# Running the context stage and the mamba projections of a four-layer cross-attention kernel in turns on each engine

## Chip, cores and metric

The kernel runs on one core of one Trainium2 chip. The metric is device time in microseconds (us) of that core; times of one execution come from its hardware profile.

## What is computed

Four layers run one after another on x (4 batches, 512 positions, width 256), all reading the same context ctx (4, 512, 256). In the first, a mamba block stands ahead of the attention. Cut to what matters here:

```python
# L0, mamba block: DI = 512, 8 heads of 64, state 128, convolution over 4 positions
zxbcdt = rms(x, norm_w) @ in_proj_w                  # 256 -> 512 (z) + 768 (xBC) + 8 (dt)
dt  = softplus(dt_raw + dt_bias)
xBC = silu(conv_b + sum(padded[:, k:k + L] * conv_w[:, k] for k in range(4)))
h_t = exp(dt * A) * h + (dt * xh) B_t ;  y_t = h_t C_t + D_skip * xh
x   = x + rms(y * silu(z), gnorm_w) @ out_proj_w
# L0..L3, cross attention: keys and values of each layer from ctx
#   L0: ctx @ Wk, ctx @ Wv   L1: the same kind   L2: ln(ctx)*g+b   L3: ln(ctx)*g1+beta1
# then L3's recurrence s = silu(s A') + u over 512 positions, plus mean(probs) @ W_prog'
```

## The kernel before

One program is written by hand for each engine: blocks for SyncE (L320), POOL (L364), ScalarE (L428), VectorE (L700) and TensorE (L1061). Each engine does its instructions in the order written, and named semaphores join them; so the order of the work is the order of these programs. Work is tiled in 16 tiles (NT) of 128 positions: 4 batches (NB) by 4 chunks (NCH). Stages stand one behind the other:

- Start. SyncE loads the first part of the packed weights (par0, the context weights), the four context blocks, the four x blocks, and then the other two parts of the weights (par_rest). POOL loads the mask and probs. TensorE takes the mean of probs (L1068) and its product (L1072); VectorE makes three bf16 parts of the mask row (L705 to L715) and the row of the mean (L717). Only then does TensorE begin the context (it waits for mod_dve 7). SyncE copies the mask parts into 12 rows (L334).
- Context, 16 tiles. TensorE turns the raw tile and the normalized one (L1094, through the helper at L1077), and makes all layers' keys (proj_T, L1084) and values (proj, L1091). ScalarE evacuates the turned tiles (ctx_ev, L435) and part of the keys and values (ctx_rows, L447); VectorE norms the context two tiles ahead (ctx_norm, L735; its root is taken by POOL, L376), and evacuates the rest (L743, L752). SyncE stores keys and values to HBM from two buffers. In between VectorE squares and scales the rows of x (L759, L772) and at tile 8 folds norm weights into projection weights (weights, L779). A tile uses four PSUM banks, two tiles all eight. The turn of a tile waits for c_dve, VectorE's last copy of two tiles before.
- Projections and convolution, 24 items: for each batch six groups of 128 channels by 512 positions. The normalized x is turned (L1137), copied by both engines (L471, L811), multiplied by the weights (L1160, into eight banks in turn), and after two items all 16 tiles' time steps are made in one run of matmuls 8 columns wide (L1146). For each item ScalarE copies it into a padded buffer (L491) and multiplies by the last tap (L492), VectorE adds the three other taps (L854), ScalarE applies SiLU (L483). There are NF = 5 buffers. VectorE makes the softplus of all time steps (L814 to L842) after three items.
- Scan over 16 chunks of tiles (L1163 on for TensorE, L500 to L547 for ScalarE, L857 to L899 for VectorE): ScalarE masks dt*A (L502), TensorE makes the decays (L1176), ScalarE exponentiates (the first use is L513), and so on.
- Attention for all layers, then the recurrence. Ahead of it POOL clears the pads of four value buffers (L400), and SyncE starts loading keys and values when that is done.

Of the kernel before, what the change touches and what calls it, by code (L numbers as in the profile page):

```python
# [8 lines left out]
BF16 = mybir.dt.bfloat16  # L9
# [5 lines left out]
P = 128  # L15
NB = 4
# [153 lines left out]
def build(nc, x, ctx_in, probs, maskf, pack, kd, vd, out):  # L170
    with ExitStack() as stack:
# [30 lines left out]
        XT = CX[:, :, :].rearrange("p a d -> p (a d)").rearrange("p (k b t) -> p k b t", k=KD, b=NB)  # L202
# [20 lines left out]
        arena = sb("arena", [P, 17920])  # L223
# [11 lines left out]
        a0 = Carve(arena[:, :])  # L235
        NX = a0.take(NT * D).rearrange("p (a d) -> p a d", a=NT)
        KS = [a0.take(KG * P).rearrange("p (g n) -> p g n", g=KG) for _ in range(2)]
        VS = [a0.take(VW) for _ in range(2)]
        cT = [[a0.take(KD * P).rearrange("p (k n) -> p k n", k=KD) for _ in range(3)] for _ in range(2)]
        cn = [a0.take(D) for _ in range(2)]  # L240
        keep = a0.take(T)
        pb = a0.take(NB * NCH * S3).rearrange("p (b k s) -> p b k s", b=NB, k=NCH)
        early = a0.take(6 * T)[0:1, :]
        m_row = early[:, 0:T]
        m_tmp = early[:, T:4 * T].rearrange("p (i n) -> p i n", i=3)
        m_part = early[:, 4 * T:6 * T].bitcast(BF16)[:, 0:3 * T].rearrange("p (i n) -> p i n", i=3)
# [6 lines left out]
        NF = 5  # L253
        xpad = [a1.take(T + CONV - 1) for _ in range(NF)]
        acc = [a1.take(T) for _ in range(NF)]
        dts = UTraw[:, 0:12 * NT * HM].rearrange("p (i a h) -> p i a h", i=12, a=NT)
# [3 lines left out]
        a2 = Carve(arena[:, rest:])  # L260
# [21 lines left out]
        Vs = [a3.take(NCH * (D + 16)).rearrange("p (k n) -> p k n", k=NCH) for _ in range(4)]  # L282
# [17 lines left out]
        ident = w("ident")  # L300

# [19 lines left out]
        def _(sp):  # L321
            sp.dma_start(W[:, CUTS[0]:CUTS[1]], pack[:, CUTS[0]:CUTS[1]]).then_inc(sem("par0"), 16)
            for b in range(NB):
                sp.dma_start(CX[:, b * NCH:(b + 1) * NCH, :], ctx_in[b].rearrange("(k p) d -> p k d", p=P)
                             ).then_inc(sem(f"cin{b}"), 16)
            for b in range(NB):
                sp.dma_start(res_by_b[:, :, b, :], x[b].rearrange("(k p) d -> p k d", p=P)
                             ).then_inc(sem(f"xin{b}"), 16)
            for i in range(1, 3):
                sp.dma_start(W[:, CUTS[i]:CUTS[i + 1]], pack[:, CUTS[i]:CUTS[i + 1]]).then_inc(sem("par_rest"), 16)  # L330
            sp.wait_ge(sem("mod_dve"), 6)
            for i in range(3):
                for g in range(4):
                    sp.dma_start(m_rows[32 * g + i:32 * g + i + 1, :], m_part[0:1, i, :]).then_inc(sem("mask_rows"), 16)  # L334

            for k in range(NT):
# [3 lines left out]
                sp.dma_start(vd[b, :, kt, :], VS[k % 2]).then_inc(sem(f"c_st{k % 2}"), 16)  # L340
            for s in range(2):
# [23 lines left out]
        def _(pool):  # L365
            pool.dma_start(keep.bitcast(I32), maskf.partition_broadcast(P)).then_inc(sem("early_in"), 16)
            pool.dma_start(m_row[:, :].bitcast(I32), maskf.rearrange("(a n) -> a n", a=1)).then_inc(sem("early_in"), 16)
            pool.dma_start(pb, probs.rearrange("b (k p) s -> p b k s", p=P)).then_inc(sem("early_in"), 16)
            pool.memset(Hst[:, :, :], 0.0)
            pool.memset(R2[:, :, :], 0.0)  # L370
            pool.memset(at2[:, :], 0.0)
            pool.memset(ones_b[:, :], 1.0).then_inc(sem("zeroed"), 1)

# [5 lines left out]
            for k in range(NT + 2):  # L379
                if k < NT:  # L380
                    root(st[k % 2][:, 9:10], st[k % 2][:, 8:9], "c", k + 1)
                if k >= NCH and (k - 2) % NCH == NCH - 1:
# [7 lines left out]
            for i in range(2):  # L390
                pool.wait_ge(sem(f"c_st{i}"), 32 * NT // 2)
# [1089 lines left out]
```

## Time and profile before

| | |
|---|---|
| median of 3 runs | 1637.56 us (1636.14 to 1640.12) |
| the profiled execution, its own time | 1636.14 us |
| its span | 1634.3 us |
| busy share of the span | TensorE 87%, ScalarE 68%, VectorE 65%, POOL 4% |
| mean granted TensorE clock | 0.944 of full speed |
| context stage | about 21 to 148 us |
| projections and convolution | about 148 to 230 us |
| scan | about 230 to 430 us |

A profile row names engine (PE is TensorE's matmuls, PEld its weight loads, DVE VectorE, ACT ScalarE, SP SyncE), line, operation and the tiles written and read. An fp32 matmul of the program shows as two records. "xN" is a number of instructions. In brackets stands the idle time of the engine ahead of a row and who ended it.

### The profile page before, as it was taken

To read this page: it belongs to the slowest core of one execution; us is meant where nothing else is said; L and a number is where in the kernel's file an instruction comes from. 1 tells how busy PE (TensorE), PEld (TensorE's weight loads), DVE (VectorE), ACT (ScalarE), POOL (GpSimd) and SP (SyncE) were. 2 spreads that over 40 slices of the span, in tenths; PEclk is the share of its full clock that TensorE was granted. 3 is DMA by queue.
4 is the path that set the end of the run, shared out by engine and by line. 5 is a ranking of instruction groups with operands and counts; after the bars stand their busy time and mean duration, and the time that the engine had idled before them with its cause. 6 is when DMAs were issued, how large, how long until landed. Compare 5 with 4: busy or idle time off the path is not lost.

```text
span 1634.3 us, 35969 instructions
## 1 busy us (share of the span) xinstructions
PE 1418.8 (87%) x13354; PEld 1031.5 (63%) x13354; DVE 1065.0 (65%) x2382; ACT 1114.4 (68%) x3382; POOL 64.6 (4%) x121
## 2 busy tenths in 40 slices
PE   5888939999789988999988999998889999888666
PEld 4787425666566655667766667776666777666444
DVE  2344776666477877867777776777777687777100
ACT  2343667888577888777778767778777777887322
POOL 1010000000100000000000000000000000000000
PEclk9999869999799999999999999999999999999655
DMA  9342000000212202212111221211022121010000
GB/s 330 115 133 93 0 0 0 2 0 1 103 41 76 69 27 64 86 38 75 54 43 37 68 64 40 66 53 53 27 79 66 40 79 53 27 53 2 7 20 26
DMA packets 67677, 90.43 MB, mean 55 GB/s; under 512 B 3440, under 2 KB 56688, under 8 KB 67120
## 3 DMA queue, kind: packets, MB, share of 16 engines
q1 hardware_dynamic: 67248, 87.34, 16.7%
q8 instruction: 108, 1.77, 0.5%
q0 software_dynamic: 256, 0.79, 0.2%
q14 instruction: 65, 0.53, 0.1%
HBM read 71.33 MB, written 16.78 MB: 54 GB/s over the span
## 4 chain that ended last, share of the span: by engine, by line
PE 58%; ACT 18%; DVE 12%; issue 10%; DMA 1%; POOL 1%; ACTq 0%; DVEq 0%; POOLq 0%
PE ps L1077 14%; PE ps L1318 10%; PE ps L1344 8%; PE ps L1084 7%; PE ps L1091 6%; DVE arena L1018 4%; PE ps L1303 3%; PE ps L1383 3%; ACT arena L639 3%; ACT dAm L502 2%; PE ps L1176 2%; DVE arena L854 2%; ACT arena L646 1%; ACT L608 1%; ACT R L698 1%
## 5 line engine op out<-in xcount | busy, mean ns | idle before, releaser
L1077 PE MATMUL ps<-W,arena 128*128 128x128 f32 x2928 | 439.2, 283 | 31.5 <-ACT arena L639 17.7
L1077 PEld LDWEIGHTS ps<-W,arena 128*128 128x128 f32 x2928 | 335.4, 148 | 180.0 <-issue 132.0
L639 ACT ACTIVATE arena<-ps,nmax 128x512 f32<-128x512 f32 x640 | 434.3, 685 | 2.1 <-DVE nmax L998 1.6
L646 ACT COPY arena<-ps 128x512 f32<-128x512 f32 x320 | 187.0, 584 | 212.7 <-PE ps L1077 208.5
L998 DVE TENSOR_REDUCE nmax<-ps 128x1 f32<-128x512 f32 x320 | 206.2, 686 | 122.0 <-PE ps L1318 82.3
L1018 DVE COPY arena<-ps 128x512 f32<-128x512 f32 x320 | 213.9, 687 | 24.2 <-PE ps L1077 11.1
L1318 PE MATMUL ps<-W,arena 32*128 32x512 f32 x1280 | 184.7, 645 | 34.8 <-DVE arena L1018 34.2
L1344 PE MATMUL ps<-arena 128*32 128x128 f32 x5120 | 172.9, 276 | 31.8 <-ACT arena L646 31.6
L1001 DVE TENSOR_REDUCE nmax<-ps 128x2 f32<-128x1024 f32 x160 | 193.8, 1211 | 0.0
L1344 PEld LDWEIGHTS ps<-arena 128*32 128x32 f32 x5120 | 130.0, 109 | 69.2 <-ACT arena L646 59.2
L1084 PE MATMUL ps<-arena,W 128*128 128x128 f32 x1152 | 153.2, 284 | 6.2 <-ACT arena L561 5.7
L1091 PE MATMUL ps<-W,arena 128*128 128x256 f32 (+1 forms) x608 | 148.5, 379 | 4.0 <-ACT arena L602 3.3
L1084 PEld LDWEIGHTS ps<-arena,W 128*128 128x128 f32 x1152 | 140.6, 197 | 12.5 <-ACT arena L561 11.6
L1303 PEld LDWEIGHTS ps<-R,at 128*128 128x128 f32 x768 | 115.6, 190 | 46.5 <-DVE R L981 25.1
L1303 PE MATMUL ps<-R,at 128*128 128x4 f32 x768 | 128.5, 238 | 6.2 <-DVE R L981 6.1
L639 ACT ACTIVATION_READ_ACCUMULATOR arena<-ps,nmax 128x1 f32 x640 | 130.4, 204 | 0.0
L1091 PEld LDWEIGHTS ps<-W,arena 128*128 128x128 f32 x608 | 104.0, 192 | 21.2 <-issue 6.1
L981 DVE SCALAR_TENSOR_TENSOR R<-th,ps 64x4 f32<-64x4 f32 x384 | 56.9, 148 | 88.9 <-ACT th L631 84.4
L376 POOL TENSOR_TENSOR st<-st,W 128x1 f32<-128x1 f32 x80 | 43.9, 548 | 1158.5 <-DVE st L727 1158.5
L1318 PEld LDWEIGHTS ps<-W,arena 32*128 32x128 f32 x1280 | 53.7, 185 | 52.1 <-issue 39.8
L631 ACT ACTIVATE th<-ps 64x4 f32<-64x4 f32 x384 | 64.0, 167 | 15.4 <-PE ps L1303 13.6
L1383 PE MATMUL ps<-R,W 64*64 64x4 f32 x256 | 47.5, 254 | 30.8 <-ACT R L698 30.8
(201 smaller groups left out, 1522.0 us busy)
## 6 DMA issues: line engine op xcount, KB each, us to landing
W<-keys SPq DMA_DIRECT2D x48, 512.0 KB, 3.7
arena<-values SPq DMA_DIRECT2D x48, 512.0 KB, 4.8
keys<-arena SPq DMA_DIRECT2D x16, 448.0 KB, 3.3
values<-arena SPq DMA_DIRECT2D x16, 448.0 KB, 3.9
W<-keys SPq DMA_DIRECT2D x16, 256.0 KB, 2.8
arena<-values SPq DMA_DIRECT2D x16, 256.0 KB, 3.2
W<-in_pack SPq DMA_DIRECT2D x1, 3180.0 KB, 18.1
W<-in_pack SPq DMA_DIRECT2D x1, 2246.0 KB, 10.1
```

The costliest lines, as they stand in the source:

```text
L639: nc.scalar.activation(Pr[:, a, :], ps[:, a, :], ACT.Exp, bias=nmax[:, u % 32:u % 32 + 1], accum_out=den[:, u % 32:u % 32 + 1]).then_inc(s ...
L646: nc.scalar.copy(PT[:, (4 * Q + a) % 8, :, :].rearrange("p k n -> p (k n)"), psT).then_inc(sem("u_ev_act"), 1)
L998: nc.vector.tensor_reduce(nmax[:, (u + g) % 32:(u + g) % 32 + 1], ps[:, g, :], AX, ALU.max, negate=True).then_inc(sem("u_mx"), 1)
L1001: nc.vector.tensor_reduce(nmax[:, u % 32:u % 32 + 2], ps[:, 2:4, :], AX, ALU.max, negate=True).then_inc(sem("u_mx"), 1)
L1018: nc.vector.tensor_copy(PT[:, (4 * Q + a) % 8, :, :].rearrange("p k n -> p (k n)"), ps[:, a, :]).then_inc(sem("u_ev_dve"), 1)
L1077: ins = nc.tensor.transpose(dst[:, k * P:(k + 1) * P], src[:, k * P:(k + 1) * P], ident)
L1084: ins = mm(dst[:, g * P:(g + 1) * P], w(wname, KD)[:, kk, g * P:(g + 1) * P], src[:, kk, :], start=kk == 0, stop=kk == KD - 1)
L1091: ins = mm(dst, src[:, kk, :], w(wname, parts)[:, kk, at_col:at_col + n], start=kk == 0, stop=kk == parts - 1)
L1303: mm(psR[:, NB * j:NB * (j + 1)], at2[:, :], R2[:, j, :], start=False, stop=True, skip_group_check=True).then_inc(sem("r_z"), 1)
L1318: ins = mm(ps[:, g, :], qT[b][rows, q, :], Ks[G % 4][rows, l.key_group(q), :], start=True, stop=l is not L0)
L1344: ins = mm(psT[32 * g:32 * g + 32, 0:P], Vs[G % 4][:, kt, first:first + 32], PT[:, (4 * Q + g) % 8, kt, :], start=kt == 0, stop=kt == NCH - 1)
L1383: mm(psR[0:S3, NB * j:NB * (j + 1)], W[0:S3, a3:a3 + S3], R2[0:S3, j, :], start=False, stop=True, skip_group_check=True).then_inc(sem("e_z ...
```

## The change

The context stage and the projections become one stage. In each engine's loop over the 16 context tiles, tile k = 4b + at carries a piece of batch b: at 0 the turn of the normalized x of that batch (half between the tile's keys and values, half behind the values), at 1 to 3 two items each, one in either place. The time steps of a batch stand behind the tile with at = 1, in four runs in place of one. PSUM is dealt anew: three banks for each of two context sides, and banks 6 and 7 (item) for the items. The turn of a tile waits for c_act (ScalarE's value copy) and no longer for c_dve. The norm weight mnorm is applied when the turned x is evacuated, no longer to the weights. NF is 4. The context's buffers move into the space of the attention weights, which are loaded after the last context store (par_late); VectorE's preparations from them (late_weights) stand at chunk 8 of the scan. The first context block is loaded before par0. Probs are loaded on SyncE's queue and summed by POOL, and the mean and its product stand behind tiles 2 and 3; the mask parts are made in tile 3. The softplus stands in tiles 14 and 15, in the last one between two convolutions. The value buffers lose their pads, and POOL's memset of them goes.

```diff
@@ SyncE
-            sp.dma_start(W[:, CUTS[0]:CUTS[1]], pack[:, CUTS[0]:CUTS[1]]).then_inc(sem("par0"), 16)
-            for b in range(NB):
-                sp.dma_start(CX[...], ctx_in[b]...).then_inc(sem(f"cin{b}"), 16)
...
+            load_ctx(0)
+            sp.dma_start(W[:, CUTS[0]:CUTS[1]], pack[:, CUTS[0]:CUTS[1]]).then_inc(sem("par0"), 16)
+            load_x(0)
+            sp.dma_start(W[:, CUTS[1]:CUTS[2]], pack[:, CUTS[1]:CUTS[2]]).then_inc(sem("par1"), 16)
+            load_ctx(1)
+            load_x(1)
+            sp.dma_start(pb, probs.rearrange("b (k p) s -> p b k s", p=P)).then_inc(sem("pb_in"), 16)
+            for b in range(2, NB):
+                load_ctx(b)
+                load_x(b)
...
+                if k == 3:
+                    sp.wait_ge(sem("mod_dve"), 6)
...
+            sp.dma_start(W[:, CUTS[2]:CUTS[3]], pack[:, CUTS[2]:CUTS[3]]).then_inc(sem("par_late"), 16)
             sp.wait_ge(sem("m_x1"), NT)
-            sp.wait_ge(sem("zeroed"), 3)
@@ POOL
+            for k in range(NT):
+                if k + 2 < NT:
+                    c_root(k + 2)
+                if k % NCH == NCH - 1 and k + 1 < NT:
+                    x_root(k // NCH + 1)
+                if k == 0:
+                    sum_probs()
+                if k == 4:
+                    pool.wait_ge(sem("mod_mm"), 1)
+                    pool.memset(Hst[:, :, :], 0.0).then_inc(sem("zeroed"), 1)
...
-            for v in Vs:
-                ins = pool.memset(v[:, :, P:], 0.0)
-            ins.then_inc(sem("zeroed"), 1)
@@ ScalarE
             ctx_ev(0)
             for k in range(NT):
+                if k:
+                    keep_item(k - 1, 1)
                 if k + 1 < NT:
                     ctx_ev(k + 1)
-                ctx_rows(k)
...
+                if k:
+                    silu(k - 1, 0)
+                ctx_keys(k)
+                if k % NCH == 0:
+                    keep_xT(k // NCH)
+                keep_item(k, 0)
+                if k:
+                    silu(k - 1, 1)
+                ctx_values(k)
+                if k == NT - 2:
                     act.wait_ge(sem("m_soft"), 3)
                     nc.scalar.activation(dts[:, 3, :, :], dts[:, 2, :, :], ACT.Exp).then_inc(sem("m_exp"), 1)
+                    nc.scalar.activation(negA[:, :], w("alog"), ACT.Exp).then_inc(sem("m_exp"), 1)
...
             act.wait_ge(sem("m_soft"), 19)
             masked_dA(0)
+            keep_item(NT - 1, 1)
+            silu(NT - 1, 0)
+            silu(NT - 1, 1)
@@ VectorE
+            ctx_norm(0)
+            ctx_norm(1)
...
+            for c in range(NCH):
+                x_square(c)
+            x_rows(0)
+            dve.wait_ge(sem("par1"), 16)
+            dve.wait_ge(sem("zeroed"), 2)
+            for k in range(NT):
+                b, at = divmod(k, NCH)
+                if k == NCH:
+                    mod_rows()
+                if at == 1:
+                    keep_xT(b)
+                if at == 2:
+                    time_steps(b)
+                ctx_keys(k)
+                if k + 2 < NT:
+                    ctx_norm(k + 2)
+                if k:
+                    conv(k - 1, 1)
+                if k == 3:
+                    mask_parts()
+                if k == NT - 2:
+                    softplus_front()
+                if k == NT - 1:
+                    softplus()
+                conv(k, 0)
+                if at == NCH - 1 and b + 1 < NB:
+                    x_square(NCH * (b + 1) + at)
+                    ctx_values(k)
+                    x_rows(b + 1)
+                else:
+                    ctx_values(k)
+                    if b + 1 < NB:
+                        x_square(NCH * (b + 1) + at)
+                if k == NT // 2:
+                    out_weights()
+            conv(NT - 1, 1)
@@ VectorE, scan
+                if k == NT // 2:
+                    late_weights()
@@ TensorE
             def ctx_turn(k):
-                    pe.wait_ge(sem("c_dve"), k - 1)
+                    pe.wait_ge(sem("c_act"), k - 1)
...
+            def items(k, j):
+                b, at = divmod(k, NCH)
+                if at == 0:
...
+                    for c in range(NCH):
+                        ins = nc.tensor.transpose(item[j][:, c * P:(c + 1) * P], NX[:, c, j * P:(j + 1) * P], ident)
+                    ins.then_inc(sem("xt_tp"), 1)
+                    return
+                f = number(item_of(k, j))
+                if at == 1:
+                    pe.wait_ge(sem("xt_act"), b + 1)
...
+                else:
+                    pe.wait_ge(sem("m_fa"), f - 1)
...
+                for kk in range(KD):
+                    ins = mm(item[j], inw[:, kk, DI + g * P:DI + (g + 1) * P], XT[b][:, kk, :], start=kk == 0, stop=kk == KD - 1)
+                ins.then_inc(sem("m_in"), 1)
...
             ctx_turn(0)
             for k in range(NT):
                 if k + 1 < NT:
                     ctx_turn(k + 1)
-                ctx_project(k)
+                ctx_keys(k)
+                items(k, 0)
+                ctx_values(k)
+                items(k, 1)
+                if k % NCH == 1:
+                    time_steps(k // NCH)
...
-                    if k == 0:
-                        pe.wait_ge(sem("m_silu"), NB * XG)
+                    if k < NB:
+                        pe.wait_ge(sem("m_silu"), XG * (k + 1))
```

## Rows read from the trace of the kernel before

**Rows 1.** Stretches: length, busy PE, PEld, DVE, ACT, POOL, clock, DMA share, GB/s.

```profile
40.00:60.00 20.00, 17.45 (x125) 15.60 (x124) 7.30 (x27) 8.19 (x24) 2.11 (x3) 1.00 0.37 122
200.00:220.00 20.00, 7.90 (x17) 2.60 (x15) 19.36 (x28) 16.05 (x27) 0.00 (x0) 0.83 0.00 0
220.00:240.00 20.00, 7.67 (x19) 4.84 (x20) 9.30 (x15) 11.43 (x25) 0.00 (x0) 0.50 0.00 0
```

**Rows 2.** Timeline of the start: start us, us, engine, line, operation.

```profile
14.48 3.55 PE L1068 MATMUL ps<-W,arena 128*64 128x1 f32 x32 [14.48 <-DMA arena<-in_probs]
14.79 0.41 DVE L705 TENSOR_SCALAR arena<-arena 1x512 f32<-1x512 int32 x1
...
17.56 0.41 DVE L715 CAST arena<-arena 1x512 bf16<-1x512 f32 x1
...
20.64 3.79 SPq L334 DMA_DIRECT2D m_rows<-arena  x6
...
21.14 0.69 PE L1077 MATMUL ps<-W,CX 128*128 128x128 f32 x2 [0.52 <-DVE cm L717]
```

**Rows 3.** Chain of waits, context: start us, us, what.

```profile
25.79 4.80 PE ps L1084 x28
...
34.49 0.66 PE ps L1077 x4
35.15 3.13 PE ps L1084 x28
38.28 3.06 PE ps L1091 x16
42.17 0.66 PE ps L1077 x4
```

**Rows 4.** DMA issues before 260 us: out<-in, count, KB each, us to landing.

```profile
W<-in_pack SPq DMA_DIRECT2D x1, 3180.0 KB, 18.1
W<-in_pack SPq DMA_DIRECT2D x1, 2246.0 KB, 10.1
```

**Rows 5.** Timeline of the mamba projections, convolution and the scan's opening.

```profile
148.49 3.69 PE L1137 MATMUL ps<-W,arena 128*128 128x128 f32 x32 [1.16 <-DVE arena L757]
...
171.19 1.28 ACT L483 ACT_TABLE_LOAD   x1
...
176.44 0.23 DVE L825 TENSOR_SCALAR UT<-UT 128x128 f32<-128x128 f32 x1 [2.12 <-ACT UT L498]
...
181.87 0.29 DVE L842 TENSOR_TENSOR UT<-UT,negA 128x128 f32<-128x128 f32 x1
...
182.07 47.11 DVE L854 SCALAR_TENSOR_TENSOR arena<-arena,W 128x512 f32<-128x512 f32 x63
...
229.75 2.43 ACT L502 ACTIVATE dAm<-W,UT 128x128 f32<-128x128 f32 x8
...
237.19 0.19 ACT L513 ACTIVATE dec<-ps 128x24 f32<-128x24 f32 x1 [3.71 <-PE ps L1179]
```

**Rows 6.** The stretch 176 to 200 us, instructions of L1160 alone.

```profile
176.00:200.00 24.00, 24.00 (x57) 10.64 (x56) 1.00 0.00 1
```

**Rows 7.** Stretches of 2 us in and after the time steps (L1146).

```profile
158.00:160.00 2.00, 2.00 (x20) 2.00 (x20) 1.93 (x4) 0.50 (x1) 0.00 (x0) 1.00 0.00 0
162.00:164.00 2.00, 2.00 (x12) 2.00 (x11) 0.00 (x0) 0.00 (x0) 0.00 (x0) 0.50 0.00 0
170.00:172.00 2.00, 2.00 (x3) 0.68 (x3) 0.76 (x2) 1.98 (x3) 0.00 (x0) 0.50 0.00 0
```

**Rows 8.** Chain of waits, first masked products of the scan's chunks.

```profile
232.32 3.75 PE ps L1176 x4
...
260.43 1.98 PE ps L1176 x4
...
272.00 1.98 PE ps L1176 x4
```

**Rows 9.** Timeline behind the scan: POOL's memsets of the value pads.

```profile
430.77 2.13 POOL L400 MEMSET arena<- 128x576 f32 x4 [6.66 <-DVE RES L884]
```

More of the change, by code:

```diff
@@ L300, in build, with item_of, number @@
         ident = w("ident")
+        side = [[ps[:, 3 * s + i, :] for i in range(3)] for s in range(2)]
+        item = [ps[:, 6, :], ps[:, 7, :]]
+        def item_of(k, j):
+            b, at = divmod(k, NCH)
+            return None if at == 0 else (b, 2 * (at - 1) + j)
+        def number(bg):
+            return bg[0] * XG + bg[1]
         block = stack.enter_context(nc.Block())
@@ L372, in _ @@
             pool.memset(ones_b[:, :], 1.0).then_inc(sem("zeroed"), 1)
+            for i in range(NF):
+                ins = pool.memset(xpad[i][:, 0:CONV - 1], 0.0)
+            ins.then_inc(sem("zeroed"), 1)
             def root(dst, src, name, n):
@@ L1120, in _, with time_steps @@
+            def time_steps(b):
+                pe.wait_ge(sem("m_fa"), b * XG + 1)
+                for c in range(NCH):
+                    for kk in range(KD):
+                        ins = mm(item[0][:, c * HM:(c + 1) * HM], XT[b][:, kk, c * P:(c + 1) * P], inw[:, kk, DI + XBC:],
+                                 start=kk == 0, stop=kk == KD - 1)
+                ins.then_inc(sem("m_dt0"), 1)
             ctx_turn(0)
@@ L1163, in _ @@
-            pe.wait_ge(sem("m_fa"), NB * XG)
+                ctx_keys(k)
[4 more added lines that the diff above has]
+                    time_steps(k // NCH)
+                if k == 2:
+                    pe.wait_ge(sem("m_fa"), 3)
+                    pe.wait_ge(sem("mod_pb"), NCH - 1)
+                    for b in range(NB):
+                        ins = mm(item[0][0:S3, b:b + 1], pbs[:, b, :], w("inv512"), start=True, stop=True)
+                    ins.then_inc(sem("mod_mm"), 1)
@@ L1164, in _ @@
+                if k == 3:
+                    pe.wait_ge(sem("m_fa"), 5)
+                    a = PLAN["wprog3"][0]
+                    mm(item[0][S3:S3 + NB, 0:D], pmT[:, :], W[0:S3, a:a + D], start=True, stop=True).then_inc(sem("mod_mm"), 1)
+            pe.wait_ge(sem("c_act"), NT)
+            pe.wait_ge(sem("c_dve"), NT - 1)
+            pe.wait_ge(sem("zeroed"), 3)
+            pe.wait_ge(sem("weights"), 1)
             for k in range(NT + 1):
                 r, X = rooms[k % 2], bank[k % 2]
+                if k == 1:
+                    pe.wait_ge(sem("c_dve"), NT)
+                    pe.wait_ge(sem("m_fa"), NB * XG)
```

373 lines of the change are left out of this document (172 added, 201 removed).

## The prediction

> **What bounds the kernel now.** I read the stretches of 20 us first, because the change stops where the chunk loop of the scan begins. In 40 to 60 us, pure context, TensorE is busy 17.45 of 20 us, ScalarE 8.19 and VectorE 7.30; in 200 to 220 us, the convolution, it is the other way round: VectorE 19.36, ScalarE 16.05, TensorE 7.90; in 220 to 240 us TensorE does little and its granted clock is 0.50 [rows 1]. So a TensorE-bound stage stands ahead of a VectorE-bound one, and each leaves idle what the other needs.
>
> The timeline of the start shows a third piece. The mean-of-probs matmuls begin at 14.48 us, released by the transfer of probs, and the first context transpose only at 21.14, behind them and their additions [rows 2]. The chain of waits gives one context tile: turn 0.66, keys 3.13, values 3.06, next turn at 42.17 after 34.49. The period is 7.68 us and the TensorE work 6.85; the 0.83 between is the wait of the turn for VectorE's last copy (c_dve) [rows 3].
>
> **What the change moves, with its price.** The total of TensorE's work stays nearly as it is; the question is what the merged stage costs if TensorE carries it.
>
> Start. par0 landed 10.1 us after its issue [rows 4], which stands at the very start, so near 10.8. It now stands behind the first context load, 512 KB; at the rate that its 2246 KB in 10.1 us make, that is at most 2.3 us more, and less since the probs no longer run beside it. I take 12.3 for the first turn, bounds 11 to 14.5. From the first turn to the first keys took 25.79 - 21.14 = 4.65 us [rows 2, 3]; ScalarE's first table load, which came before it until now, adds one of 1.28 [rows 5]: keys at about 18.3. VectorE meanwhile does two norms, four squares and four row scalings, and waits for par1, which stands behind x of batch 0; I estimate its first keys copy at 22, just when TensorE has done the first keys, whose slow first block takes 4.80 [rows 3].
>
> The loop on TensorE. Tile 0 costs 4.8 + 3.06 and two groups of transposes. The 32 transpose records of four batches took 3.69 us [rows 5], so 0.92 a batch: tile 0 ends at about 27. Fifteen more tiles at 6.85, the last without a turn: 102.1. The turn now waits for ScalarE's c_act, not c_dve, so the 0.83 is dropped. Projections: 57 records in 24 us of full clock [rows 6], 0.43 each, four to an item, 1.71; 24 items make 41.1. Transposes of three batches 2.8. Time steps: 20 records in 2 us at clock 1.00 [rows 7], 64 records make 6.4. Mean-of-probs, now a few matmuls in tiles 2 and 3: 1.6, an estimate. Sum 27 + 102.1 + 41.1 + 2.8 + 6.4 + 1.6 = 181.
>
> Do the other two keep up? A tile with two items costs TensorE 6.85 + 3.42 = 10.3 us. ScalarE: 8.19 x 7.68 / 20 = 3.15 of context a tile, and for an item's copy, multiply and SiLU 16.05 x 2.24 / 20 = 1.8 by the stretch of the convolution [rows 1], twice: 6.75. VectorE: 7.30 x 7.68 / 20 = 2.8 of context a tile, and per item three multiply-adds, 47.11 / 63 = 0.75 each [rows 5], so 2.24, twice: 7.3, with handoffs and the extra rows up to 10 in the last tile of a batch. Both are under 10.3. In their orders I follow one tile from TensorE's turn at 0: keys half done at 2.0, item 0 at 5.5, its copies on ScalarE at 6.9, VectorE's second convolution of the tile before at 7, its SiLU 7.6, value copy 8.1, next turn at 10.3. The tightest wait has 2 us of slack. One place breaks it: in tile 3 VectorE also does the six mask operations (14.79 to 17.97 us at the start of before [rows 2], 3.2), and tile 4 is a short one (7.8 us on TensorE), so c_act comes late: some 3 us, once. For switching between the shapes and short handoffs I add 1 more. TensorE ends at 185.
>
> Tail. In the last tile VectorE carries the softplus chain, from 176.44 to 182.16 before [rows 5], 5.7 us, between two convolutions. The last tile starts at 185 - 9.6 = 175.4; VectorE: keys 177.5, convolution 179.8, softplus and negA 186, convolution and values 189. ScalarE waits for the softplus, does the masked dA (2.43 [rows 5]) to 188.4, and only then evacuates the last item, 189.8; its convolution ends 192, SiLU 192.7, table load for the exponential 1.28. So the first decay exponential comes at about 194 where it came at 237.19 [rows 5]: 43.2 us earlier. VectorE and ScalarE hold this end, not TensorE.
>
> Scan opening. The first masked product took 3.75 us at half clock, and 1.98 from 260.43 on, in a period of 272.00 - 260.43 = 11.57 [rows 8]. TensorE now idles some 3 us before it and not 24, so the opening is worth between 0 and 3 us; I take 1, between the two, since the gap is shorter but not gone. The Trainium skill (TensorE: Matmul & The Clock Gate, "What's actually happening") says that an idle engine falls back to half clock; by it alone this 1 us would be 0. The trace agrees that it falls in the long gap (0.50 [rows 1]) and has no gap of this length.
>
> Moved past the queues. The attention weights (3180 KB, 18.1 us to land [rows 4]) are issued behind the last context stores; their first reader is VectorE in chunk 8 of the scan, 8 x 11.57 = 93 us later, so they cost nothing; if that cover were gone it would be those 18 us. The four small preparations there are under 1 us on VectorE, while ScalarE's chain sets that loop: 0, bound 1. The 12 mask-row DMAs now stand in SyncE's queue between tiles 3 and 4, 3.79 us for six of them before [rows 2], done before store 4 is ready. POOL has three additions in front of its root for tile 3, due a tile later, and the 2048-wide memset behind a root; 0, bounds 0 and 2. Behind the scan, POOL's four memsets of the value pads, 2.13 us [rows 9], stood before the roots of the first queries: 1.5 off, as the roots still wait for their statistics.
>
> Sum: 43.2 + 1 + 1.5 = 45.7 off the profiled execution's own 1636.1, so 1590.4. The median of the runs shown is 1637.6, 1.4 above that execution: 1592.
>
> **Rivals.** (a) The clock falls in the merged stage, in pieces. In the 64-record run of 8-column matmuls the grant fell from 1.00 at 158 us to 0.50 by 162 and stood at 0.50 until after 170 [rows 7]; they now come as four bursts of 16 with transposes near them. If each burst leaves about 10 us at half clock, it costs 4 to 5: 16 to 20 together, 1610. Against: the context holds 1.00 with 16 turns and a gap in each tile [rows 1]. The Trainium skill (the same page, "A second HAM failure mode: psum-queue depth-cycling") warns that small idles from cycling through PSUM banks make the clock swing; there are two item banks now in place of eight. No row here shows that in the context, though its banks cycle too. 12%.
>
> (b) The handoffs cost more than I follow: 24 items in two banks, with 0.5 to 1.5 us of waiting on each, 12 to 36 us: 1604 to 1628. For it: three engines in fixed orders; against: the slack above. 10%.
>
> (c) The stages do not overlap, since each engine waits in its turn for the slowest: then only the start (9), the pads and the clock remain: 1626. 2%.
>
> (d) Slower than before. The mixed stream never earns the full clock. At half clock an item takes 3.42, a tile's first block 4.80 where it is 3.13 [rows 3], value blocks double. Sixteen tiles at about 12 us, 82 for the items and 18 for turns of x, time steps and the rest make 292, against the 170 that I count from the first turn, so 120 more and 45 less: 1712. It decides from some 37% of the stage at half clock. Against it stands 1.00 in the context and from 176 to 200 us [rows 6]. 3%.
>
> **Numbers.** The forecast has 73%, by its own bounds (start -1.3 to +2.2, handoffs -3 to +7, opening and POOL -2 to +3) 1583 to 1601. The range for 8 in 10 takes in part of (b) and most of the small end of (a): 1583 to 1608. A measurement of this kernel can tell about 0.3%, 5 us, from no change. Faster by more than that: forecast, (a), (b), (c), 96%, as I give 1% of (c) to no change that can be told: same 1%. Slower: (d), 3%.
>
> **What would show it.** Right: the first turn at 12 to 13 us; context tiles 10 to 12 us apart where they carry items and about 8 where they don't; TensorE over 9 tenths busy at clock 1.00 to about 185; the first decay exponential near 194; scan period still 11.57; attention unchanged. Wrong: TensorE waiting for ScalarE's copies in each tile, a clock under 1.00 between 60 and 180 us, the last convolution later than 195, or a longer scan period while the attention weights load.

## The result and the profile after

The changed kernel takes 1588.22 us (median of four runs, 1586.30 to 1593.50) against 1638.84 for the kernel before, now also of four runs (1636.14 to 1643.59): ratio 0.9703, with a 95% interval of 0.9679 to 0.9727. The forecast was 1592.0, in a range of 1583 to 1608. The profiled execution took 1586.75 us; its span is 1585.0 and its mean granted clock 0.957, where before had 1634.3 and 0.944.

First the stretches of 20 us of the kernel after, with the columns of [rows 1]:

```profile
core 0: us, PE busy (x) PEld busy (x) DVE busy (x) ACT busy (x) POOL busy (x), PEclk, DMA share, GB/s
20.00:40.00 20.00, 20.00 (x127) 17.38 (x127) 8.62 (x25) 8.20 (x20) 3.28 (x5) 1.00 0.75 211
60.00:80.00 20.00, 16.00 (x99) 13.95 (x98) 12.97 (x33) 9.24 (x24) 3.86 (x4) 0.91 0.30 93
160.00:180.00 20.00, 20.00 (x117) 15.63 (x117) 12.54 (x25) 12.78 (x26) 0.00 (x0) 1.00 0.28 92
180.00:200.00 20.00, 15.66 (x47) 9.03 (x46) 12.48 (x28) 12.14 (x31) 0.00 (x0) 0.74 0.42 149
```

TensorE is busy nearly all of the time at clock 1.00, with VectorE at 12 to 15 and ScalarE at about 12 of 20 us beside it once items run. The stretches between 20 and 180 us that are not shown have 19.84 to 20.00 us of TensorE at 1.00. One stretch is different, 60 to 80 us; it is read below. So the merged stage is TensorE-bound, where [rows 1] showed one stage bound by TensorE and one by VectorE.

The timeline of the start of after answers to [rows 2]:

```profile
11.91 0.69 PE L1156 MATMUL ps<-W,CX 128*128 128x128 f32 x2 [11.91 <-DMA W<-in_pack]
14.79 1.28 ACT L469 ACT_TABLE_LOAD   x1 [14.79 <-PE ps L1156]
17.91 4.36 PE L1163 MATMUL ps<-W 128*128 128x128 f32 x19 [1.39 <-ACT W L472]
20.98 0.42 DVE L796 TENSOR_TENSOR W<-ps,UT 128x256 f32<-128x256 f32 x1 [1.01 <-PE ps L1163]
```

The first turn waits for par0, the table load lies between it and the keys, and the keys come 6.0 us behind the turn.

A tile with two items and one with the half turns of x, from the timeline of after (it answers to [rows 3]), with the last value copies of ScalarE (L488, c_act) and VectorE (L805, c_dve):

```profile
85.54 0.42 PE L1156 MATMUL ps<-W,CX 128*128 128x128 f32 x2
86.01 3.29 PE L1163 MATMUL ps<-W 128*128 128x128 f32 x28
89.13 1.88 PE L1229 MATMUL ps<-CX,W 128*128 128x512 f32 x4
90.85 3.21 PE L1170 MATMUL ps<-W 128*128 128x256 f32 x16
92.86 0.46 ACT L488 COPY W<-ps 128x384 f32<-128x384 f32 x1
93.90 1.88 PE L1229 MATMUL ps<-CX,W 128*128 128x512 f32 x4
94.93 0.41 DVE L805 TENSOR_TENSOR W<-ps,W 128x256 f32<-128x256 f32 x1
95.61 0.38 PE L1156 MATMUL ps<-W,CX 128*128 128x128 f32 x2
...
105.66 0.38 PE L1156 MATMUL ps<-W,CX 128*128 128x128 f32 x2
...
113.45 0.44 PE L1156 MATMUL ps<-W,CX 128*128 128x128 f32 x2 [0.15 <-ACT W L488]
```

From turn to turn the first takes 95.61 - 85.54 = 10.07 us, with no wait, and the second 113.45 - 105.66 = 7.79. ScalarE's copy is done at 93.32, 2.3 us before the turn that needs it, VectorE's at 95.34, only 0.3 before.

The one place in the loop where TensorE stands still for long, in tile 4 and before the turn behind it (timeline of after, all engines):

```profile
64.98 0.63 PE L1212 MATMUL ps<-W,arena 128*128 128x128 f32 x4 [0.98 <-DVE cm L764]
...
66.84 1.81 POOL L429 MEMSET SS<- 128x2048 f32 x1
67.00 1.79 DVE L780 TENSOR_SCALAR W<-CX,st 128x256 f32<-128x256 f32 x1 [0.73 <-POOL st L399]
68.72 2.31 DVE L842 SCALAR_TENSOR_TENSOR arena<-arena,W 128x512 f32<-128x512 f32 x3
71.06 0.63 ACT L517 ACTIVATE arena<-arena 128x512 f32<-128x512 f32 x1 [4.72 <-DVE arena L842]
71.59 0.46 ACT L488 COPY W<-ps 128x384 f32<-128x384 f32 x1
72.11 0.44 PE L1156 MATMUL ps<-W,CX 128*128 128x128 f32 x2 [3.02 <-ACT W L488]
```

Read from the bottom: the turn waits 3.02 us for ScalarE's value copy (c_act, L488), which stands behind a SiLU that waits for VectorE's convolution, which stands behind the norm's row scaling (L780). That scaling took 1.79 us; the same instruction took 0.41 at 89.64 us. At 66.84 POOL's memset of 2048 columns began and took 1.81.

Behind the stall the clock fell. Of the stretches of 2 us of after, with the columns of [rows 1], the first row is the one at the lowest clock; the two below it are the turn that ends the stall and the next one in the timeline of "again", a second execution of the same kernel that is read in the next section:

```profile
74.00:76.00 2.00, 2.00 (x11) 2.00 (x11) 1.14 (x5) 0.58 (x2) 0.00 (x0) 0.50 1.05 330
...
72.55 0.44 PE L1156 MATMUL ps<-W,CX 128*128 128x128 f32 x2 [3.02 <-ACT W L488]
84.35 0.41 PE L1156 MATMUL ps<-W,CX 128*128 128x128 f32 x2
```

From that turn to the next, after takes 85.54 - 72.11 = 13.43 us, "again" 84.35 - 72.55 = 11.80. The same stall stood ahead of both, and only after paid 1.6 us more in clock.

The end of the stage (timeline of after; it answers to [rows 5]):

```profile
182.95 1.88 PE L1229 MATMUL ps<-CX,W 128*128 128x512 f32 x4
185.22 0.29 DVE L893 TENSOR_TENSOR UT<-UT,negA 128x128 f32<-128x128 f32 x1 [0.39 <-DVE negA L890]
185.55 2.44 ACT L544 ACTIVATE dAm<-W,UT 128x128 f32<-128x128 f32 x8 [3.29 <-DVE UT L893]
187.90 0.56 ACT L505 COPY arena<-ps 128x512 f32<-128x512 f32 x1
188.14 2.60 PE L1280 MATMUL ps<-dAm,W 128*128 128x512 f32 x4 [3.31 <-ACT dAm L544]
189.17 2.32 DVE L842 SCALAR_TENSOR_TENSOR arena<-arena,W 128x512 f32<-128x512 f32 x3 [0.76 <-ACT arena L506]
191.53 0.63 ACT L517 ACTIVATE arena<-arena 128x512 f32<-128x512 f32 x1 [1.87 <-DVE arena L842]
192.18 1.28 ACT L558 ACT_TABLE_LOAD   x1
193.47 0.19 ACT L558 ACTIVATE dec<-ps 128x24 f32<-128x24 f32 x1
```

The chain is the one of the forecast: softplus, masked dA (L544), the last item's copy, its convolution, its SiLU, the table load, the first decay exponential. That comes at 193.47 us instead of 237.19.

Where the 49.3 us of span went, by four marks in each trace (first decay exponential; last addition of the mamba block to x; first and last score of the attention):

| | before | after | difference |
|---|---|---|---|
| start to first decay exponential | 237.2 | 193.5 | -43.7 |
| to the last addition to x | 193.1 | 192.9 | -0.2 |
| to the first score | 11.8 | 11.0 | -0.8 |
| first score to last score | 1067.0 | 1063.7 | -3.3 |
| last score to the end | 125.2 | 123.9 | -1.3 |

The last two lines are in code that the change does not touch. Cut into stretches of 50 us, before has five in the attention with a granted clock of 0.97, after one; and in the 20 us behind the last score the clock is 0.87 before and 0.96 after.

### The profile page after: what moved, and what is told of

Read it like the earlier page. It is cut to its first block, busy times and chain, and to the rows that moved or that the text cites. A ratio compares the mean times of both kernels' runs of the same rounds, so it can differ in the third digit from the quotient of the medians.

```text
span 1585.0 us, 35918 instructions
## 1 busy us (share of the span) xinstructions
PE 1401.9 (88%) x13330; PEld 1023.4 (65%) x13330; DVE 1064.8 (67%) x2383; ACT 1113.8 (70%) x3382; POOL 63.3 (4%) x118
## 3 DMA queue, kind: packets, MB, share of 16 engines
q1 hardware_dynamic: 69312, 87.87, 17.4%
q8 instruction: 107, 1.75, 0.5%
## 4 chain that ended last, share of the span: by engine, by line
PE 60%; ACT 19%; DVE 11%; issue 9%; DMA 1%; POOL 0%; ACTq 0%; DVEq 0%; POOLq 0%; SPq 0%
PE ps L1156 14%; PE ps L1424 10%; PE ps L1450 8%; PE ps L1163 8%; PE ps L1170 6%; DVE arena L1105 4%; PE ps L1409 3%; PE ps L1489 3%; ACT arena L686 3%; ACT dAm L544 2%; PE ps L1229 2%; PE ps L1280 2%; ACT arena L693 2%; ACT L655 1%; ACT R L745 1%
## 5 line engine op out<-in xcount | busy, mean ns | idle before, releaser
L1156 PE MATMUL ps<-W,arena 128*128 128x128 f32 x2896 | 428.9, 282 | 28.7 <-ACT arena L686 18.1
L1156 PEld LDWEIGHTS ps<-W,arena 128*128 128x128 f32 x2896 | 328.5, 147 | 175.4 <-issue 129.2
L1163 PE MATMUL ps<-arena,W 128*128 128x128 f32 x704 | 98.5, 286 | 5.8 <-ACT arena L608 5.3
L1170 PE MATMUL ps<-W,arena 128*128 128x256 f32 x352 | 97.1, 399 | 4.0 <-ACT arena L649 3.3
L1163 PEld LDWEIGHTS ps<-arena,W 128*128 128x128 f32 x704 | 87.2, 196 | 11.4 <-ACT arena L608 11.2
L1170 PEld LDWEIGHTS ps<-W,arena 128*128 128x128 f32 x352 | 61.6, 193 | 16.7 <-issue 5.9
## 6 DMA issues: line engine op xcount, KB each, us to landing
W<-in_pack SPq DMA_DIRECT2D x1, 2246.0 KB, 10.6
```

What stands on the lines that cost most here:

```text
L1156: ins = nc.tensor.transpose(dst[:, k * P:(k + 1) * P], src[:, k * P:(k + 1) * P], ident)
L1163: ins = mm(dst[:, g * P:(g + 1) * P], w(wname, KD)[:, kk, g * P:(g + 1) * P], src[:, kk, :], start=kk == 0, stop=kk == KD - 1)
L1170: ins = mm(dst, src[:, kk, :], w(wname, parts)[:, kk, at_col:at_col + n], start=kk == 0, stop=kk == parts - 1)
```

## The experiments

The theory: the gain is the overlap of the two stages, and what is left over it are two waits that the change made itself, the stop at tile 4 and the softplus chain in the tail. The rivals: the time in the attention is part of the effect (the value buffers without pads); the merged order runs only because its turn waits for c_act; something else in the change (start, loads, opening) carries the gain. Line numbers differ a little between the kernels, where an edit adds or takes lines. "The mark" is the start of the first decay exponential. It is counted from the start of the kernel and so carries two things that are not of an edit: the first tile, whose slow first block of keys takes 4.7 to 6.2 us whatever the edit, and the clock behind the stall, which cost 1.6 us in the profiles of after, pads, burst and loads and nothing in the other profiles of the merged order. Where it matters, the distance between two turns around the edit stands beside the mark.

**The changed kernel again.** No edit; the yardstick of the next three.

> The changed kernel as it is, once more, as the yardstick of this group. Expected: 0.970 of the kernel before, first decay exponential of the scan at 193.5 us give or take 0.5, scan period 11.57. The profile of the change was 49.3 us shorter in span, but only 43.7 of that stands at the first decay exponential and 44.7 at the first attention scores; the other 4.6 lie in the attention, which the change does not touch. Theory: they are short drops of the granted clock in the profile of before (five stretches of 50 us at 0.97 against one in the changed kernel's), so they are not of the change, and this run may show them or not. Rival: the value buffers without pads make the attention itself faster; then it shows 4 to 5 us less in the attention here too.

1589.21 us, ratio 0.9706 (0.9677 to 0.9736). The first decay exponential came at 192.3 us, outside the 193.5 give or take 0.5: the clock did not fall behind the stall. The attention took 1067.1 us, what it had taken before, again with five stretches at 0.97, one of them:

```profile
892.00:942.00 50.00, 46.10 (x488) 33.45 (x488) 36.85 (x87) 34.50 (x107) 3.29 (x6) 0.97 0.22 71
```

The same program shows 1063.7, 1067.1 and, in a third profile ("again2" below), 1070.9, so the 3.3 us are not the change's.

**The pads back.** The value buffers and POOL's memset as they were:

```diff
-        Vs = [a3.take(NCH * D)... for _ in range(4)]
+        Vs = [a3.take(NCH * (D + 16))... for _ in range(4)]
...
+            sp.wait_ge(sem("padded"), 1)
...
+            for v in Vs:
+                ins = pool.memset(v[:, :, P:], 0.0)
+            ins.then_inc(sem("padded"), 1)
```

> The pads of the value buffers and POOL's memset of them restored, with SyncE waiting for it. Theory (pads cost only their place ahead of the first roots): the first attention scores come 1 to 1.5 us later against the first decay exponential than in the run as it is, and the attention from there to the end takes the same. Rival (the layout of the value buffers matters for the attention's loads or matmuls): the attention is 4 to 5 us longer.

1592.32 us, ratio 0.9729 (0.9691 to 0.9768), an interval that overlaps that of the run above. The timeline of this kernel shows the memset ahead of the root, and the turn behind it:

```profile
385.90 0.42 DVE L975 TENSOR_TENSOR RES<-RES,ps 128x256 f32<-128x256 f32 x1 [5.67 <-PE ps L1174]
386.38 2.13 POOL L436 MEMSET arena<- 128x576 f32 x4 [6.67 <-DVE RES L975]
...
389.65 1.11 PE L1160 MATMUL ps<-W,arena 128*128 128x128 f32 x4 [3.79 <-DVE arena L784]
```

From the last addition to the first score it takes 11.6 us, against 10.6 in "again": 1.0, where I had put 1.5. The profiles without pads have 10.5 to 11.2 there and that of before 11.8, so the 1.0 is good to some half us. The attention itself took 1074.2, with nine stretches below 1.00, down to 0.90. That is more clock loss, in a place where the pads have no part; one profile of each cannot rule out a small share.

**The turn waits for c_dve again.**

```diff
-                        pe.wait_ge(sem("c_act"), k - 1)
+                        pe.wait_ge(sem("c_dve"), k - 1)
```

> TensorE's turn of a context tile waits for VectorE's last value copy again (c_dve) and not for ScalarE's (c_act). Theory: in the merged order VectorE finishes that copy 0.3 to 1 us after TensorE wants to turn, since it comes behind two convolutions, so TensorE idles in each tile with items: 12 tiles by about 1 us, 2 more in the last tile of a batch; first decay exponential 8 to 15 us later, at 202 to 208. Rival (the merged stage has slack, the wait's change was worth nothing beyond the 0.83 a tile of before): under 2 us later.

1592.41 us, 0.9725 (0.9692 to 0.9758); first decay exponential at 194.0, 1.7 us later than in "again". From the turn of tile 2 to the end of the last item it takes 158.4 us against 156.2 there, so the wait costs 2.2. My expectation was several times too high; the rival with its slack was right at the mark, if narrowly. The chain of waits of TensorE, 12 to 190 us (columns: who waited for what, us in total, times, longest):

```profile
PE ps L1156 <- DVE W L805: 6.6, 7, 2.6
```

After has 3.3, 3 times, for ScalarE's L488 there, and 1.0 for the mean's row (L764) in tile 4, which is not there in this kernel: 4.3 against 6.6. The 0.3 us between VectorE's last copy and the turn in the steady tile of after are mostly enough: later turns of this kernel wait for it 0.16 and 0.62 us. So the wait that cost 0.83 in each tile of [rows 3] costs little in the merged order with either engine named in it: the item between the values and the next turn gives the copies most of their time.

**The overlap taken out.** Everything else of the change stays (loads, sums on POOL, two item banks, per-batch norms, softplus, late weights), but for the copies of the mask rows, which go behind the context stores; each engine first does all context tiles and then all items:

```diff
@@ TensorE, and the same split in the loops of the other engines
             for k in range(NT):
                 if k + 1 < NT:
                     ctx_turn(k + 1)
                 ctx_keys(k)
-                items(k, 0)
                 ctx_values(k)
+            for k in range(NT):
+                items(k, 0)
                 items(k, 1)
```

> Same instructions, but in two passes: all 16 context tiles, then all items (start, loads, PSUM banks and evacuation with the norm weight as in the changed kernel; mask rows are copied behind the context stores). Nothing overlaps. Theory (the overlap is the gain): context ends near 18 + 16 x 7 = 130, then the items go at VectorE's 2.24 us each, 24 of them 54, with transposes, time steps and softplus some 80 in all as before: first decay exponential at 215 to 228, 22 to 34 us later than in the run as it is; total 0.985 to 0.993 of before. Rival (most of the gain is the earlier start and the removed waits): under 12 us later.

1636.63 us, ratio 0.9989 (0.9970 to 1.0008), and the first decay exponential at 239.8: 47 us later, more than the 22 to 34 I expected. The context ended about 126 us, so the better start is there; but the items alone then took 114 us to the mark, against 89 in before (148.5 to 237.2). Two waits of TensorE in them, from the timeline of this kernel:

```profile
152.49 1.94 PE L1211 MATMUL ps<-W,arena 128*128 128x128 f32 x8 [8.20 <-DVE cm L765]
179.24 1.94 PE L1211 MATMUL ps<-W,arena 128*128 128x128 f32 x8 [5.91 <-DVE arena L827]
```

The chains of a batch (the mean's row at 152, squares, root and rows of x at 179) have nothing beside them and stand open, and the granted clock is 0.50 from 150 to 160 us. So without the overlap the other parts together give nothing that can be told from no change, and with it they give 3%: the gain is the overlap, which also pays for costs that the other parts have on their own.

**Mask parts and their rows two tiles later** (in tile 5 in place of 3):

```diff
-                if k == 3:
+                if k == 5:
                     mask_parts()
```

> The six mask operations of VectorE and the mask-row DMAs stand in tile 5 instead of tile 3, nothing else. In the profile of the change TensorE idles 0.98 us ahead of the transposes of tile 4 and 3.02 ahead of the turn at 72.11, for ScalarE's value copy, which waits for a SiLU behind VectorE's late convolution. Theory (the mask operations make VectorE late there, tile 5 has room): both idles all but vanish, first decay exponential 3 to 5 us earlier than in the run as it is (192.3 to 193.5), so 188 to 190. Rival (tile 4 is short, so the lateness comes with the batch's end anyway, or goes on to tile 5 or 6): under 1.5 us earlier.

1589.26 us, 0.9711 (0.9677 to 0.9744); first decay exponential at 189.0, 3.3 us earlier than in "again". The wait of the turn for L488 at 69.3 us is down from 3.02 to 1.53, and the 0.98 for L764 is gone. From the turn of tile 5 to that of tile 6 it is 2.7 us shorter; the other 0.6 lie in the first tile, which the edit does not touch. The total cannot show a gain of this size: its interval is 5 us wide to either side, and the attention took 1071.2 us in this profile, as it did in one of the unchanged kernel (1070.9).

**POOL's 2048-column memset two roots later.**

```diff
-                if k == 4:
+                if k == 6:
                     pool.wait_ge(sem("mod_mm"), 1)
                     pool.memset(Hst[:, :, :], 0.0).then_inc(sem("zeroed"), 1)
```

> POOL's memset of the scan's state (128 x 2048) stands behind its root for tile 8 instead of tile 6, nothing else. In the profile of the change the VectorE row L780 beside that memset (66.84 to 68.65 us) took 1.79 us where it takes 0.41 elsewhere, ahead of the longest wait of TensorE. Theory (VectorE and POOL hold each other up while the memset runs, and 1.4 us of the 4 us of idle in tile 4 come of it): the slow L780 moves to the next place beside the memset, some 20 us later, and costs nothing there; first decay exponential 1 to 1.5 us earlier. Rival (that row waited for something else, TensorE's reading of the buffer): L780 stays slow at 67 us and nothing moves.

1585.91 us, 0.9681 (0.9657 to 0.9705); mark at 190.1, 2.2 us earlier than in "again", of which 1.4 stand between the turns of tiles 5 and 6 and 0.9 in the first tile. The timeline of this kernel, at the old place and at the new one:

```profile
66.58 0.41 DVE L780 TENSOR_SCALAR W<-CX,st 128x256 f32<-128x256 f32 x1 [0.73 <-POOL st L399]
...
86.07 1.80 POOL L429 MEMSET SS<- 128x2048 f32 x1
86.23 1.79 DVE L780 TENSOR_SCALAR W<-CX,st 128x256 f32<-128x256 f32 x1 [0.74 <-POOL st L399]
```

The long row scaling went with the memset. That shows whose it is: a VectorE instruction that starts 0.16 us after the memset ends 0.15 us after it (86.23 + 1.79 = 88.02 against 87.87), and where there is no memset it takes 0.41. The Trainium skill (SBUF — State Buffer, "SBUF: two separate sides") has the pair of ports that VectorE and GpSimd share as an exclusive lock held for a whole instruction; the trace agrees that the row ends with the memset, to 0.15 us. The 1.4 us between the turns are the 1.79 - 0.41 of the row.

**The softplus one tile earlier**, in tile 14 whole, and its exponentials on ScalarE ahead of that tile's evacuations:

```diff
+                if k == NT - 2:
+                    softplus_front()
                 ctx_keys(k)
...
                 if k == NT - 2:
-                    softplus_front()
-                if k == NT - 1:
                     softplus()
```

> The softplus is made a tile earlier: its front right behind the last time steps, the exponentials on ScalarE before the first SiLU of tile 14, the chain on VectorE between the convolutions of tile 14 instead of tile 15. Theory (VectorE holds the tail with 6 us of softplus, ScalarE's masked dA and its last item wait for it): last item evacuated right behind TensorE, first decay exponential 2.5 us earlier, near 190; TensorE idles 1 us or less ahead of the scan instead of 3.3, so it keeps the full clock through the opening and the first period of the scan is 11.6 to 12.5 us instead of 14.0; together 3.5 to 5 us by the first attention scores. Rival (the tail moves into tile 14 and TensorE waits there): under 1 us.

1584.63 us, 0.9677 (0.9654 to 0.9701); mark at 189.3, 3.0 earlier than in "again", all of it behind the end of the last item. Its timeline:

```profile
183.55 1.95 PE L1280 MATMUL ps<-dAm,W 128*128 128x512 f32 x4
...
187.97 1.28 ACT L558 ACT_TABLE_LOAD   x1
189.51 0.33 PE L1290 MATMUL ps<-W,arena 128*128 128x128 f32 x1 [2.95 <-ACT dec L558]
```

The masked product has no wait and takes 1.95 us at full clock, as the theory had it. (It took 1.95 in mask5 too, behind a wait of 3.31; behind the same wait the other profiles have 2.60 to 3.75.) But TensorE then waits 2.95 us for the exponential instead of 3.31 for the masked dA, and the clock still falls (0.57 at 190 to 194): from the mark to the last addition it takes 192.1 us, as in "again" (192.2). That part of the theory, a faster opening of the scan, missed.

**All time steps in one run**, behind tile 13, as it was in before; four runs of 16 become one of 64:

```diff
-                if k % NCH == 1:
-                    time_steps(k // NCH)
+                if k == NT - 3:
+                    for b in range(NB):
+                        time_steps(b)
```

> The time steps of all four batches stand in one run of 64 matmul records of 8 columns behind tile 13, instead of four runs of 16. Same instructions. Theory of the clock (it falls in a long run of such matmuls, as in the kernel before, where it went from 1.00 to 0.50 some 5 us after the run began and stayed for about 10): the grant shows 0.50 for a stretch behind 165 us, the run takes 8 to 9 us instead of 4 times 1.7, and the first decay exponential comes 4 to 8 us later. Rival (the fall in the kernel before came of the idle gaps around it, not of the narrow matmuls): clock stays 1.00 and the end moves by less than 1 us.

1595.31 us, 0.9755 (0.9710 to 0.9799); mark at 198.4, 6.1 later than in "again". The clock behind the stall fell here as in after, so 1.6 of them are not the edit's; against after it is 4.9. Stretches of 4 us of this kernel, columns as above:

```profile
156.00:160.00 4.00, 4.00 (x26) 2.99 (x24) 1.65 (x4) 1.27 (x2) 0.00 (x0) 1.00 0.28 78
160.00:164.00 4.00, 4.00 (x31) 4.00 (x31) 0.00 (x0) 0.00 (x0) 0.00 (x0) 0.79 0.45 155
164.00:168.00 4.00, 4.00 (x20) 4.00 (x21) 0.34 (x4) 0.00 (x0) 0.00 (x0) 0.50 0.00 0
168.00:172.00 4.00, 4.00 (x21) 4.00 (x20) 0.98 (x5) 2.30 (x6) 0.00 (x0) 0.50 0.00 0
```

The run stands from 157.96 to 167.6 us. TensorE never idles in it, and yet the clock falls to 0.50 within it and stays there for the next tile's keys, 5.30 us instead of 3.29. The four short runs of after, 1.85 us each, stand in stretches at 1.00. So rival (a) had a real ground in what a long run does, and with the run split into four it stays away.

**The changed kernel once more**, the yardstick of the last two.

> The changed kernel as it is, as the yardstick of this group: 0.970 of the kernel before, first decay exponential at 192.3 to 193.5 us.

1587.21 us, 0.9705 (0.9681 to 0.9729), mark at 192.4; the attention took 1070.9 us, with six stretches of 50 us below 1.00, down to 0.93.

**The three together**: mask parts in tile 5, memset at root 6, softplus in tile 14.

> Mask operations in tile 5, POOL's memset behind its root for tile 8, and the softplus a tile earlier, all three together. Each alone moved the first decay exponential by 2.2 to 4 us (192.3 as it is; 189.0, 190.1, 189.3). Theory: the first two share the 4 us of idle around tile 4, so together they give at most that 4 and not 5.5; the softplus acts on the tail and adds its own 3: 185 to 186, and a ratio to before of 0.963 to 0.967. Rival: without the stall in tile 4 the next one (VectorE's mask work in tile 5, the batch's end at tile 8) comes up and gives half of it back: 187 to 188.

1580.99 us, 0.9650 (0.9624 to 0.9676), 6.2 us below "again2"; mark at 185.1, 7.3 earlier. At the mark the edits gave 3.3, 2.2 and 3.0 alone, 8.5 in sum. Around the stall they add up better (timelines of the four kernels, us):

| | turn of tile 5 | turn of tile 6 | between | shorter than "again" |
|---|---|---|---|---|
| again | 60.65 | 72.55 | 11.90 | |
| mask parts in tile 5 | 60.07 | 69.30 | 9.23 | 2.67 |
| memset at root 6 | 59.79 | 70.32 | 10.53 | 1.37 |
| all three | 60.45 | 68.31 | 7.86 | 4.04 |

The first two share one stall and its 4.0 us, and take exactly 2.7 and 1.4 of it, alone or together; with the softplus' 3.0 in the tail that is 7.0, and the rest of the 7.3 lies in the first tile. What is left of it in TensorE's waits from 12 to 190 us of this kernel, and of the tail:

```profile
PE ps L1290 <- ACT dec L558: 3.0, 1, 3.0
...
PE ps L1156 <- ACT W L488: 0.5, 3, 0.2
```

**The old order of loads**: par0 first, then the four context blocks, the four blocks of x, par1, probs.

```diff
-            load_ctx(0)
             sp.dma_start(W[:, CUTS[0]:CUTS[1]], pack[:, CUTS[0]:CUTS[1]]).then_inc(sem("par0"), 16)
-            load_x(0)
-            sp.dma_start(W[:, CUTS[1]:CUTS[2]], pack[:, CUTS[1]:CUTS[2]]).then_inc(sem("par1"), 16)
...
+            for b in range(NB):
+                load_x(b)
+            sp.dma_start(W[:, CUTS[1]:CUTS[2]], pack[:, CUTS[1]:CUTS[2]]).then_inc(sem("par1"), 16)
```

> The order of the loads alone is undone: par0 first, then the four context blocks, the four x blocks, and only then par1 and probs. Theory: par0 lands 1 us sooner and so does the first turn (near 11), but par1 comes behind 8.3 MB, at 24 to 27 us, VectorE's first keys copy waits for it (21 as it is), TensorE with it: first decay exponential 3 to 6 us later than as it is. Rival (the start has cover, the order is worth nothing): within 1 us.

1596.75 us, 0.9754 (0.9726 to 0.9781), mark at 198.9: 6.5 later than in "again2", a little over the 3 to 6 expected; but 1.6 of them are the clock behind the stall, which fell here and not there, and 4.9 are left for the loads. The waits from 5 to 30 us of this kernel:

```profile
PE ps L1152 <- DMA CX<-in_ctx: 12.5, 1, 12.5
DVE W L792 <- DMA W<-in_pack: 5.5, 1, 5.5
PE ps L1166 <- DVE W L794: 2.8, 1, 2.8
```

The first turn is only 0.6 to 0.8 us later (12.5). The loss is VectorE's, which waits 5.5 us for par1 at the end of the queue, and then TensorE's for VectorE. The new order of the loads is worth those 5 us to the merged kernel, since its start has no slack for what VectorE needs; what it would give to the kernel before was not run.

## Why the prediction was right

**Start.** First turn 11.91 (forecast 12.3), keys 17.91 (18.3), VectorE's first keys copy 20.98 (22). Each is 0.4 to 1.0 early; the turn is within its bounds of 11 to 14.5.

**The loop.** A tile with two items takes 10.07 us (forecast 10.3), a short one 7.79 (7.8); TensorE's last item ends at 182.95 + 1.88 = 184.8 (185). The tile is a sum of records of [rows 3], [rows 5] and [rows 6], and held to some 2%, because TensorE found its inputs ready. (24 us for the 57 records of [rows 6] is 0.42 each and not the 0.43 of the sum; the item's 1.72 us from one group to the next in after, 89.13 to 90.85, bears out the 1.71 all the same.)

**The slack.** "The tightest wait has 2 us of slack" held: 2.3 us in the tile shown. The stall around tile 4 was forecast at 3 us by the mask operations and a late c_act; it was 3.02 + 0.98 = 4.0, and only part of it is theirs: moving the mask took 2.7 us out of it, moving the memset 1.4. The step that was mis-sized is "the 2048-wide memset behind a root; 0, bounds 0 and 2". It holds VectorE for 1.4 us (1.79 - 0.41), in the one tile without slack. The clock then fell to 0.50 behind the stall in this profile, 1.6 us that the sum did not have either. That TensorE's end came within 0.2 us of the forecast is therefore partly luck: the tiles with items took 2 us less than summed and the 1 us for handoffs was hardly used, against 1.0 more stall, 1.6 of clock and 0.6 for the time steps (a tile with them takes 1.75 us more, and the sum had 1.6).

**The wait for c_dve.** I took 0.83 a tile off for it. In the merged order it is worth 2.2 us in all. The term was no error in the sum, since the tile without wait is what runs in both; but the reason given, the other semaphore, was not the cause: the items are.

**Tail.** 193.47 (194), with the chain as told. **Opening.** 1 us was taken, out of bounds of 0 and 3: 0.2 in this profile, 0.9 in "again" (192.2 against 193.1). TensorE waits 3.31 us, and the product takes 2.60 us, where 3.75 and 1.98 were the two levels of [rows 8]. From the mark to the last addition the profiles of all kernels have 192.1 to 193.3 us, the one with the product at full clock (mask5) 193.3, and before 193.1: whether the shorter gap is worth anything there is not shown. The scan's period is 11.6 us as before. **Boundary.** 1.5 taken, 0.8 and 1.0 measured, give or take half a us.

**The sum.** The forecast for the profiled execution was 1590.4, and it took 1586.75. The steps answer for 0.5 early at the mark, 0.8 and 0.7 too much for opening and boundary; the other 4.6 us lie in the attention and behind it, where the granted clock was higher than in before; executions of one program differ in it by more than that (1063.7 to 1070.9 us). The "1592" thus leans on a clock like before's; the three medians of the changed kernel are 1588.2, 1589.2 and 1587.2. One sum of the prediction is wrong: the bounds it lists, 6.3 down and 12.2 up around 1592, make 1586 to 1604 and not 1583 to 1601. The measured median lies in either.

**The rivals.** (a), the clock falling behind each run of time steps, did not happen, and the run in one piece shows that it was near. It did fall once, behind the stall and not behind a run, for 1.6 us; a clock under 1.00 between 60 and 180 us was one of my signs of being wrong, and it came in a small way. The warning of the Trainium skill (TensorE: Matmul & The Clock Gate, "A second HAM failure mode: psum-queue depth-cycling") on cycling PSUM banks that I set beside it did not come about: with two item banks and six of the context the clock was 1.00 in every stretch of 20 us up to 180 but the one with the stall. But it speaks of small idles, and TensorE had hardly any here, so this is no test of it. (b), handoffs of 0.5 to 1.5 us on each item, falls with waits of 0.2. (c) did not happen; built on purpose it came to 1636.6 and not to its 1626, as I had not counted that the chains of a batch stand open once nothing covers them, nor the clock lost beside them; what two item banks in place of eight cost there was not tried by itself. (d) falls with the clock of 1.00.

## What to carry to other kernels

Two stages that wait for different engines can be laid beside each other by hand, if one tile of the merged order is followed on each engine and every chain has its slack; the price can then be read from the records of the two stages to a few per cent. The gain left on the table was in the single pieces of work put into one tile (a mask, a memset, a softplus chain): put each where the next tile is a long one, and look also at what POOL does beside VectorE. Judge small gains by the distance between two marks that stand closely around the edit: a mark counted from the start moved by up to 1.2 us between executions of one program here, and the total carries the clock of the rest as well.

## What the hardware did that I had not expected

- A VectorE row scaling of 128x256 took 1.79 us in place of 0.41, for as long as a POOL memset of 128x2048 (1.80 to 1.81) ran beside it, at each of the places to which the memset was moved (64, 67, 84 and 86 us), and 0.41 again where it had left.
- In a run of 64 matmul records 8 columns wide the granted clock fell from 1.00 to 0.50 with TensorE busy all the time; in runs of 16 between wide ones it did not.
- Behind one and the same stall of 4 us the granted clock fell to 0.50 in one execution of the changed kernel (74 to 76 us) and stayed at 1.00 in two others. It is worth 1.6 us.
- Executions of the same program differ by up to 7.2 us in the attention alone (1063.7, 1067.1 and 1070.9), where some stretches of 50 us have a granted clock of 0.97 or 0.93. What sets these off is open; nothing was tried for it.
